# A GNN kernel on one core: tiles 2 to 4 of x also read in a transposed layout, their means spread by TensorE and subtracted on GpSimd, the bias loaded and added earlier

## The reference

```python
h = jnp.maximum(_layernorm(x, axis=-1), 0.0)
# inside the first layer:
var = jnp.mean(jnp.square(h), axis=-1, keepdims=True)
norm_x = ln_weight * (h * jax.lax.rsqrt(var + 1e-6))
out = norm_x @ W_root + bias
for r in range(2):                     # two kinds of edges
    msg = norm_x[src] @ W_rel[r] * w_r[:, None]
    out = out + segment_sum(msg, dst) / maximum(cnt_r, 1)[:, None]
x = x + h + elu(out) @ wo_weight
```

## Time and profile before

| what | value |
|---|---|
| time, median of 3 runs | 509.95 us (509.91 to 511.46) |
| time of the profiled execution | 512.07 us |
| its span | 510.3 us |
| TensorE busy | 490.9 us, 96% |
| DVE busy | 372.3 us, 73% |
| ACT busy | 227.5 us, 45% |
| GpSimd busy | 78.7 us, 15% |
| granted TensorE clock, mean | 0.998 of full speed |

### The profile page before, as it was taken

The page is one execution under the profiler, slowest core; times in us unless marked ns, Lnnn a source line. Parts: engine busy times, 40 slices in busy tenths (PEclk is TensorE's granted clock), DMA queues, the critical chain, the costliest instruction groups (busy, mean ns, idle before and its releaser), DMA issues.

```text
span 510.3 us, 7733 instructions
## 1 busy us (share of the span) xinstructions
PE 490.9 (96%) x2953; PEld 422.5 (83%) x2953; DVE 372.3 (73%) x635; ACT 227.5 (45%) x382; POOL 78.7 (15%) x81
## 2 busy tenths in 40 slices
PE   3998999999999999999999999999999999999995
PEld 2888999988899999998778888888887878878785
DVE  4846786599989999997965555556598878777634
ACT  5855444415866666668632222234233323323211
POOL 1092223200000000002000000000083333322400
PEclk9999999999999999999999999999999999999999
DMA  8964254413012335237921111100022232222211
GB/s 254 234 186 139 80 169 142 126 39 99 16 41 86 101 93 166 82 120 260 324 71 40 41 40 44 38 1 0 1 80 82 81 93 70 80 82 80 81 43 45
DMA packets 22187, 49.15 MB, mean 96 GB/s; under 512 B 4799, under 2 KB 10710, under 8 KB 22019
## 3 DMA queue, kind: packets, MB, share of 16 engines
q1 hardware_dynamic: 20879, 44.66, 29.5%
q0 software_dynamic: 1264, 3.93, 2.2%
HBM read 33.05 MB, written 16.85 MB: 98 GB/s over the span
## 4 chain that ended last, share of the span: by engine, by line
PE 78%; DVE 7%; issue 5%; DMA 4%; ACT 3%; POOL 1%; SPq 0%; ACTq 0%; DVEq 0%; POOLq 0%
PE ps L1330 9%; PE ps L1598 9%; PE ps L1600 9%; PE ps L1599 9%; PE ps L1495 7%; PE ps L1579 7%; PE ps L1580 7%; PE ps L1581 7%; PE ps L1399 4%; PE ps L1418 2%; PE ps L1551 2%; DMA xt<-xh_scratch 1%; DMA x_scratch<-xt 1%; PE ps L1553 1%; PE ps L1552 1%
## 5 line engine op out<-in xcount | busy, mean ns | idle before, releaser
L1598 PE MATMUL ps<-h_hi,att_hi 125*125 125x512 f32 (+1 forms) x190 | 73.6, 387 | 0.0
L1599 PE MATMUL ps<-h_lo,att_hi 125*125 125x512 f32 (+1 forms) x190 | 72.7, 382 | 0.0
L1600 PE MATMUL ps<-h_hi,att_lo 125*125 125x512 f32 (+1 forms) x190 | 72.6, 382 | 0.0
L1579 PE MATMUL ps<-wg,gT_hi 128*125 128x512 f32 x160 | 63.8, 399 | 0.6 <-DVE wg L1096 0.6
L1580 PE MATMUL ps<-wg,gT_hi 128*125 128x512 f32 x160 | 63.1, 394 | 0.0
L1581 PE MATMUL ps<-wg,gT_lo 128*125 128x512 f32 x160 | 63.1, 394 | 0.0
L1495 PE MATMUL ps<-msg_hi,adj_hi 125*125 125x288 f32 x180 | 50.3, 304 | 0.8 <-ACT adj_hi L612 0.8
L1495 PE MATMUL ps<-msg_lo,adj_hi 125*125 125x286 f32 x180 | 45.9, 295 | 0.0
L699 ACT ACTIVATE em<-ps,rinv 125x512 f32<-125x512 f32 (+1 forms) x21 | 14.0, 668 | 63.1 <-DVE hp L1201 63.1
L1600 PEld LDWEIGHTS ps<-h_hi,att_lo 125*125 125x125 f32 x190 | 35.3, 186 | 8.0
L1598 PEld LDWEIGHTS ps<-h_hi,att_hi 125*125 125x125 f32 x190 | 35.3, 186 | 7.8
(11 more groups left out here) (216 smaller groups left out, 1080.0 us busy)
## 6 DMA issues: line engine op xcount, KB each, us to landing
xt<-in_x SPq DMA_DIRECT2D x10, 448.0 KB
xh_scratch<-xt SPq DMA_DIRECT2D x10, 448.0 KB
xt<-xh_scratch SPq DMA_DIRECT2D x10, 448.0 KB
x_scratch<-xt SPq DMA_DIRECT2D x10, 448.0 KB
x1t<-x_scratch SPq DMA_DIRECT2D x10, 448.0 KB
xr<-x_scratch SPq DMA_DIRECT2D x10, 448.0 KB
out_x<-xr SPq DMA_DIRECT2D x19, 224.0 KB
wg_raw<-in_L_gnn_W POOLq DMA_DIRECT2D x7, 512.0 KB, 7.4
```

The costliest lines, as they stand in the source:

```text
L1579: M.matmul(to, hi, wg[k][:, 0, cut], start=n == 0, stop=False)
L1598: M.matmul(to, hi[:, s, :], h_hi[:, s, cut], start=s == 0, stop=False)
L1599: M.matmul(to, hi[:, s, :], h_lo[:, s, cut], start=False, stop=False)
L1600: return M.matmul(to, lo[:, s, :], h_hi[:, s, cut], start=False, stop=s == TILES - 1)
```

## The change

The host passes x a second time as `x_by_column`: for each tile 128 columns by eight slices by 125 rows. For tiles 2, 3 and 4 the kernel loads that layout into `xc` too (`load_columns`, 512 KB each). TensorE no longer turns `ht` of these tiles: one matmul spreads the column of means over all partitions (`means_spread`), ACT copies it to SBUF (`means_out`), GpSimd subtracts it from `xc` (`centred`), ACT writes `hT_hi` = Relu(xc) (`raised`) and DVE writes `hT_lo` = max(xc, 0) - hT_hi in one instruction (`low_parts`). These rows lack the reciprocal deviation, so DVE multiplies it into the factor of the messages (`mean_square`). `norm` and `residual` of these tiles stay. The bias is loaded ahead of x's tile 2 and added behind the first `residual`, which no longer waits for it. The load of tile 4 moves ahead of the store of tile 1. Several steps change places:

```diff
--- before.py
+++ after.py
...
@@ -47,6 +47,7 @@
     FH = F // 2
     FB = F + FH + 1
     AHEAD = 4
+    COLUMNS, ROWS = 2, 5
     BAND = 112
     FP = F + 2
     CB = T + 1
...
+
+    def column(t):
+        return t - COLUMNS + 1
+
+    def turned_in(t):
+        return data(t if t < COLUMNS else t - ROWS + COLUMNS)
+
+    def by_column(t):
+        return COLUMNS <= t < ROWS
+
+    def columns_in(t):
+        return (t - COLUMNS) // 2 * 16 + 16
...
+        columns_of = ExitStack()
+        sb(columns_of, "below_xc", [P, 8256], BF16)
+        xc = [sb(columns_of, f"xc{b}", [P, KT, T], F32) for b in range(2)]
...
+        (*means,), end1 = lay(end1, *pairs_of("means", [P, T], F32))
...
-        first_tp = lambda t, h: tp_bank(6 + h if t == AHEAD - 1 else h)
+        first_tp = lambda t, h: tp_bank(h)
...
+            def load_columns(t, b):
+                if t >= COLUMNS + 2:
+                    sp.wait_ge(S["hT_lo_rdy"], data(t - 2))
+                sp.dma_start(xc[b][:], x_by_column[t]).then_inc(S["xc_in"][b], 16)
...
             for k in range(KT):
                 load_w(k)
+            sp.dma_start(bias_b[:], conv_bias.partition_broadcast(T)).then_inc(S["bias_in"], 16)
             load_x(2, 0)
+            load_columns(2, 0)
             load_x(3, 1)
-            sp.dma_start(bias_b[:], conv_bias.partition_broadcast(T)).then_inc(S["bias_in"], 16)
+            load_columns(3, 1)
             for k, ap in enumerate((src, dst, edge_type)):
                 sp.dma_start(edges_i[:, k], ap.rearrange("(g p e) -> p g e", g=CG, p=CP)).then_inc(S["edges_in"], 16)
             last_of = lambda first, n: bass.AP(dst.tensor, dst.offset + first * CP * T - 2, [[T, CP], [CP * T, n], [1, 2]])
             sp.dma_start(last_i[1:CP, 0:1, :], last_of(0, 1)[1:CP]).then_inc(S["last_in"], 16)
             sp.dma_start(last_i[:, 1:CG, :], last_of(1, CG - 1)).then_inc(S["last_in"], 16)
             store_xh(0, 0)
+            load_x(4, 0)
             store_xh(1, 1)
-            load_x(4, 0)
             load_x(5, 1)
+            load_columns(4, 0)
...
+            pool.wait_ge(S["w_split"], KT - 1)
+            def centred(t, b, d):
+                pool.wait_ge(S["means_rdy"], column(t))
+                pool.wait_ge(S["xc_in"][b], columns_in(t))
+                G.tensor_tensor(xc[b][:], xc[b][:], means[b][:].unsqueeze(1).broadcast_to([P, KT, T]), ALU.subtract).then_inc(S["cent_rdy"], 1)
+            residual(0, 0, 0)
             pool.wait_ge(S["bias_in"], 16)
             G.tensor_scalar(bias_b[:], bias_b[:], 1.0, None, ALU.add).then_inc(S["bias_rdy"], 1)
-            pool.wait_ge(S["w_split"], KT - 1)
-            for t in range(AHEAD):
-                residual(t, t % 2, t // 2)
+            centred(2, 0, 1)
+            residual(1, 1, 0)
+            centred(3, 1, 1)
+            residual(2, 0, 1)
+            residual(3, 1, 1)
+            centred(4, 0, 2)
+            residual(4, 0, 2)
             more_constants()
-            pipeline((residual, 0), steps=(AHEAD, TILES - 2))
+            pipeline((residual, 0), steps=(ROWS, TILES - 2))
...
             def norm(t, b):
                 act.wait_ge(S["rstd_rdy"], data(t))
-                act.wait_ge(S["hT_ps"], room(t))
+                if 2 <= t < COLUMNS + 2 or t >= ROWS + 2:
+                    act.wait_ge(S["hT_ps"], turned_in(t - 2))
...
             def transposed(t, b, d):
-                act.wait_ge(S["hT_ps"], data(t))
+                act.wait_ge(S["hT_ps"], turned_in(t))
...
+            def means_out(t, b, d):
+                act.wait_ge(S["spread_ps"], column(t))
+                if t >= COLUMNS + 2:
+                    act.wait_ge(S["cent_rdy"], column(t - 2))
+                A.copy(means[b][:], bank(b, P, T)).then_inc(S["means_rdy"], 1)
+
+            def raised(t, b, d):
+                act.wait_ge(S["cent_rdy"], column(t))
+                act.wait_ge(S["g_ps"], room(t))
+                A.activation(hT_hi[b][:], xc[b][:], ACT.Relu).then_inc(S["hT_hi_rdy"], 1)
...
             deviation(2, 0)
+            means_out(2, 0, 1)
             norm(2, 0)
+            messages(0, 0, 0)
+            raised(2, 0, 1)
             deviation(3, 1)
+            mean_square(2, 0)
             norm(3, 1)
-            messages(0, 0, 0)
-            transposed(2, 0, 1)
-            mean_square(2, 0)
             mean_square(3, 1)
-            normed(4, 0, 2)
-            messages(1, 1, 0)
-            pads()
-            pipeline((transposed, 1), (messages, 2), (normed, -1), steps=(AHEAD, TILES + 1))
+            for t in range(AHEAD - 1, ROWS):
+                b, d = t % 2, t // 2
+                messages(t - 2, b, d - 1)
+                means_out(t, b, d)
+                deviation(t + 1, 1 - b)
+                raised(t, b, d)
+                norm(t + 1, 1 - b)
+                mean_square(t + 1, 1 - b)
+                if t == AHEAD - 1:
+                    pads()
+            messages(ROWS - 2, 1, 1)
+            normed(ROWS + 1, 0, 3)
+            pipeline((transposed, 1), (messages, 2), (normed, -1), steps=(ROWS + 1, TILES + 1))
...
             def low_parts(t, b):
                 dve.wait_ge(S["hT_hi_rdy"], data(t))
+                if by_column(t):
+                    V.scalar_tensor_tensor(hT_lo[b][:], xc[b][:], 0.0, hT_hi[b][:].bitcast(F32), ALU.max, ALU.subtract).then_inc(S["hT_lo_rdy"], 1)
+                    return
...
             def mean_square(t):
                 dve.wait_ge(S["rm_rdy"], data(t))
-                V.reciprocal(stats1[:, bass.ds(t, 1), 5], stats1[:, bass.ds(t, 1), 5]).then_inc(S["rms_rdy"], 1)
+                if not by_column(t):
+                    V.reciprocal(stats1[:, bass.ds(t, 1), 5], stats1[:, bass.ds(t, 1), 5]).then_inc(S["rms_rdy"], 1)
+                    return
+                link(V.reciprocal(stats1[:, bass.ds(t, 1), 5], stats1[:, bass.ds(t, 1), 5]))
+                V.tensor_tensor(stats1[:, bass.ds(t, 1), 5], stats1[:, bass.ds(t, 1), 5], stats1[:, bass.ds(t, 1), 2], ALU.mult).then_inc(S["rms_rdy"], 1)
...
             deviation(2, 0)
-            moments(3, 1, 1)
+            variance(3, 1)
             dve.wait_ge(S["bias_rdy"], 1)
             messages(0, 0, 0)
             low_parts(2, 0)
+            deviation(3, 1)
             mean_square(2)
+            messages(1, 1, 0)
             moments(4, 0, 2)
-            messages(1, 1, 0)
             stage1(AHEAD, 5)
...
             def transposed(t, b, d):
                 pe.wait_ge(S["h1_rdy"], data(t))
-                if t != AHEAD - 1:
-                    pe.wait_ge(S["hT_lo_rdy"], room1(t))
+                pe.wait_ge(S["hT_lo_rdy"], room1(t))
...
+            def means_spread(t, b, d):
+                pe.wait_ge(S["var_rdy"], data(t))
+                if t < COLUMNS + 2:
+                    pe.wait_ge(S["hT_lo_rdy"], data(COLUMNS - 1))
+                else:
+                    pe.wait_ge(S["means_rdy"], column(t - 2))
+                M.transpose(bank(b, P, T), mv[b][:, 0:1].broadcast_to([T, P]), ident[0:T, 0:T]).then_inc(S["spread_ps"], 1)
...
             def stage1(first, end):
-                pipeline((transposed, 1), (products, 2), steps=(first, end))
+                pipeline((lambda t, b, d: (means_spread if by_column(t) else transposed)(t, b, d), 1), (products, 2), steps=(first, end))
...
                 products_of(1, k)
-            for k in range(2, 7):
+            for k in range(2, 5):
                 products_of(0, k)
                 products_of(1, k)
-            products_of(0, 7)
-            transposed(2, 0, 1)
-            products_of(1, 7)
+            products_of(0, 5)
+            means_spread(2, 0, 1)
+            for k in range(6, KT):
+                products_of(0, k)
+            for k in range(5, KT):
+                products_of(1, k)
             stage1(AHEAD, 8)
...
+    n_tiles, n_slices = 10, 8
+    rows, columns = inputs["x"].shape[0] // n_tiles, inputs["x"].shape[1] // n_slices
+    by_column = np.asarray(inputs["x"]).reshape(n_tiles, rows, n_slices, columns).transpose(0, 3, 2, 1)
```

More of the change, by code:

```diff
@@ L4, with rgcn_gat_kernel @@
 from contextlib import ExitStack
-def rgcn_gat_kernel(nc, x, src, dst, edge_type, ln_weight, w_rel, w_root, conv_bias, wo_weight, w_gat, a_gat, out):
+def rgcn_gat_kernel(nc, x, x_by_column, src, dst, edge_type, ln_weight, w_rel, w_root, conv_bias, wo_weight, w_gat, a_gat, out):
     F32, R32, BF16, F16 = mybir.dt.float32, mybir.dt.float32r, mybir.dt.bfloat16, mybir.dt.float16
@@ L150, in rgcn_gat_kernel @@
         first_rows_of.close()
+        columns_of = ExitStack()
+        sb(columns_of, "below_xc", [P, 8256], BF16)
+        xc = [sb(columns_of, f"xc{b}", [P, KT, T], F32) for b in range(2)]
+        columns_of.close()
         zero_adj_of = ExitStack()
@@ L194, in rgcn_gat_kernel @@
         assert end1 <= h_end and end2 <= h_end
+        (*means,), end1 = lay(end1, *pairs_of("means", [P, T], F32))
+        assert end1 <= h_end
```

(7 more changed lines are left out.)

8 lines of the change are left out of this document (4 added, 4 removed).

## The result

The changed kernel took 515.16 us (median of 5, 514.80 to 516.83) against 510.25 us for the kernel before in the same session (median of 5, 509.91 to 511.46). The ratio is 1.0091, with a 95% interval of 1.0079 to 1.0104: about 4.6 us slower. The forecast was 509.2 us with a range up to 511.8, and slower by more than 0.3% had a chance of 0.14.

A forecast was written before the change was run, and what follows sets the result against it. TensorE, busy 96% of the span, bounds the kernel; three transpose sets (3 × 0.75) plus 1.87 us idle cap the gain at 4.1. T(5) 1.3 us earlier, 0.8 kept from 509.95, gives 509.15, say 509.2; range 507.9 to 511.8.

The forecast's parts named there:

- Tiles 2 and 3: Early-stage steps: tile 2's products start at 33.3 instead of 34.99, 1.7 us ahead; tile 3's chain follows.
- case 3: Rival, faster, chance 0.17: GpSimd's subtraction takes 2.06 us or less, giving 508.4 us, or 507.8 at 1.85.
- the two combinations that the forecast left open: Tile 3's low part before or after GpSimd's residual(3), ending 43.2 or 45.6; tile 3's products end 52.7 or 55.1.
- the signs that were to show it right: Trace signs: low parts 2 us and more beside GpSimd additions, no GpSimd queue gap around tiles 3 and 4, T(5) near 55.2.
- a sign of being wrong: Trace sign against the forecast: the clock of any row up to 70 us under 1.00.
- The 2.0 us of the earlier trace: TensorE's waits up to 130 us behind DVE's hT_lo, placed as 0.45 us at tile 2's products and 1.42 at tile 4's transposes.
- L911 of tile 5: DVE's step due at 49.47, held by residual(4) to 50.9, 1.6 us later than before.
- The quotients follow: ... 2.42 us, so to 53.3: DVE from L911 of tile 5 to tile 4's low part: 2.42 us after deducting the 2.15 us L828 was held.
- T(5): Start of tile 5's transposes on TensorE, 56.51 before; forecast 55.2, 1.3 us earlier.
- Case 4: Rival, slower, chance 0.15: the pause before T(5), 4.1 or 3.0 us, lowers TensorE's clock, costing up to 2 us: 512.3.
- T(6): Start of tile 6's transposes on TensorE; forecast to wait for DVE, whose tile 6 chain loses 0 to 0.5 us.
- T(7): Start of tile 7's transposes on TensorE; forecast to wait for DVE, like T(6).

The follow-up runs named there:

- e2: Changed kernel with GpSimd's ten constants moved to its idle start, ahead of the first residual; ratio 1.0071 to the kernel before.
- e5: Changed kernel with constants and quotients early and the rest of the edge list ahead of tile 6's statistics; ratio 1.0003 to the kernel before.
- e8b: Repeat of e8, unchanged, on the same chip as e10; 509.88 us, ratio 0.9985 to the kernel before.
- e3: Changed kernel with 26 unread matmuls filling TensorE's pause before tile 5's transposes; ratio 1.0035 to the kernel before.
- b0: The kernel before, no edit, profiled once more; 510.69 us.
- b2: Kernel before with x_by_column as a further input that nothing reads; ratio 0.9997 to the kernel before.
- b3: Kernel before with the further input, its three loads and SP's changed queue order, tiles unused; ratio 1.0013 to the kernel before.
- e7: e6 with an input of only the three tiles that are read; ratio 0.9971 to the kernel before.
- e8: e6 with the full further input declared last among the inputs; ratio 0.9976 to the kernel before.
- b1: Kernel before with e6's order of work and no transposed layout; ratio 1.0014 to the kernel before.
- e10: e8 with eight unread matmuls filling the two waits ahead of tile 7's transposes; 509.03 us, ratio 0.9958 to the kernel before.
- e6: Changed kernel, constants and quotients early, tile 5's high and low part ahead of tile 6's normalisation and statistics; ratio 0.9999 to the kernel before.

## Why the prediction was wrong

**Tiles 2 and 3: right in the main.** Spread(2) at 26.48 (forecast 26.75), products(2) at 32.77 (33.3), DVE's root part of tile 1 at 36.44 (37.3), L911 of tile 4 held by 1.2 us (1.35). The subtraction takes 2.16 us and not 2.3; `residual` was the right row to choose it by, and case 3, which needed 2.06 or less, didn't come. The low part takes 1.18 to 1.20 us when free; the Relu 1.02 (1.1). Tile 3's low part went ahead of residual(3) (41.09, 1.19 us; residual(2) and (3) took 5.79 us together and not 4.8), so products(3) were through at 51.94, the early one of the two combinations that the forecast left open. Of the signs that were to show it right, two didn't come: no low part took 2 us (1.59, 1.19 and 1.20), and GpSimd's queue had gaps of 4.97 and 0.74 us ahead of the subtractions for tiles 3 and 4. The clock under 1.00, a sign of being wrong, came. The 2.0 us of the earlier trace rows were read loosely: they are three waits of transposes, the longest the 1.42; the 0.45 us ahead of products(2) isn't among them. The constants are ten instructions, not eleven.

**L911 of tile 5: right in kind.** It was held 1.2 us, to 49.8 (50.9 forecast).

**The step that failed: "The quotients follow: ... 2.42 us, so to 53.3".** They took 6.25 us, from 49.80 to 56.05: 2.0 us more for the cast beside the constants and 2.0 us more for a quotient beside residual(5). I had taken off the 2.15 us that residual(5) had cost in the old trace, because I saw it arrive only with the low part; it came at 51.98 and took one of the quotients instead of racing the low part. And I had put the constants beside the quotients at no cost to the quotients. In the old trace DVE stood idle beside them, so no row could price it. e2 prices it: cast 2.74 us with the constants beside it, 0.73 without. The Trainium skill, SBUF — State Buffer, "Who interferes with whom", has this rule: a cast or scalar operation in its two-port mode contends with any GpSimd instruction. The trace agrees, 2.0 us for nine short ones that only write. I had named the rule and drawn the wrong conclusion from it: I let the two queues take turns, by which the constants would end last. They gave DVE one turn, behind the ninth. By my own times without turns between the two: constants to 53.25, cast to 54.0, the next step held by residual(5) to 55.6 and done at 56.0, three more to 57.1, low part to 58.3. That is a T(5) of 58.4 with a pause of 5.7 us: 1.9 us later than before makes 511.8, the top of my range, and the clock comes on top of it.

**Case 4: right mechanism, wrong size and chance.** The pause before T(5) lowered the clock. It was 5.5 us long and not 4.1, because the quotients were late. The rows have the low clock behind pauses of 5.48, 5.45, 3.56 and 3.01 us; e5, with a pause of 2.50 us, has a lower mean clock in five of ten executions. The one row that the forecast had, a fall about 3.3 us after the last matmul, was a sample: in e8b's profile the fall comes 2.1 us after it, in e5's 5.1. The price was 1.38 us in e3's profile and 2.9 us by its ratio, against "up to 2 us". With the clock kept, 1.8 us of the 4.6 are left by e3's ratio, about what the later T(6) and layer 2 take; by these ratios the clock was the larger part. The loss of T(6) against b0 in the profiles is 1.0 to 1.3 us of lateness and 1.1 to 1.4 us of clock. The forecast took half speed for the first eight transposes from their 1.93 us; the clock column reads 1.00 in that stretch (0 to 21 us in the earlier trace rows), so that row didn't show it. The row that has both is T(5)'s, 1.90 us at a granted clock of 0.50.

**What no case had: 1 us in layer 2.** The forecast took it that behind T(5) the end gains what T(5) gains. In all twelve profiles of kernels with the layout in use it takes 120.4 to 121.2 us from layer 2's first product to the first with the attention, in the five without 119.4 to 120.0. TensorE waits there for DVE's split of the weights, and the chain that ended last shows what DVE had waited for, the reload of the stored sum of x and `ht`. DVE's rows, before (b0) and changed:

```profile
248.14 1.23 DVE L1081 TENSOR_TENSOR xt<-ps,xt 125x1024 f32<-125x1024 f32 x1 [0.51 <-DMA xt<-xh_scratch]
```
```profile
251.88 1.23 DVE L1147 TENSOR_TENSOR xt<-ps,xt 125x1024 f32<-125x1024 f32 x1 [1.55 <-DMA xt<-xh_scratch]
```

This wait is 1.25 to 2.08 us in the twelve and 0.31 to 0.82 in the five. POOL's loads of the weights at the same time land in 8.5 us (median from issue to landing), in b0 in 7.2; ACT waits 1.3 us for one of them, but off that chain. It is not the input (b2), not the loads or SP's order (b3), not the input's size or place (e7, e8), and not the order of the work around the list (b1). Which part of the changed program makes these loads late stays open; e10 and e8b, with landings of 7.8 and 7.6 us and still 121.2 and 120.5 us, say that the weights' landing is not the whole of it. The time behind the last matmul varies from 4.3 to 6.2 us among kernels of both kinds and is not explained either.

**The gain was there.** The forecast put the gain of T(5) by durations alone at over 2 us; e6's rows have T(5) 3.7 and T(6) 4.0 us ahead of b0 (2.5 to 4.0 and 2.8 to 4.3 ahead of the four profiles with the old order). It reached the end only in part (e8: 0.24% and, again, 0.15%; e10: 0.42%): T(7) keeps 2.8 us of it, 1 us goes in layer 2, and the clock falls in some executions.
